# Graph attention layers on one core: s_j brought along the rows by way of memory, and the leaky scores made by ScalarE in PSUM

## The reference

```
h = max(layernorm(x), 0)
for l in range(3):
    si = h @ attn_w[l, :256];  sj = h @ attn_w[l, 256:]
    scores = si[:, :, None] + sj[:, None, :] + attn_b[l]
    scores = where(scores >= 0, scores, 0.2 * scores)      # leaky
    scores = where(adj + eye > 0, scores, -inf)
    attn = softmax(scores)
    h1 = layernorm(h + attn @ h) * g1[l] + beta1[l]
    h = layernorm(h1 + gelu(h1 @ W1[l] + b1[l]) @ W2[l] + b2[l]) * g2[l] + beta2[l]
out = x + h
```

## Time and profile before

| | before |
|---|---|
| median of 3 runs | 2236.1 us |
| the profiled execution | 2237.38 us, span 2235.3 us |
| busy: PE, PEld | 2193.7, 1525.4 us |
| busy: DVE, ACT, POOL | 1767.4, 1884.1, 1886.3 us |
| chain that ended last, by engine | PE 94%, POOL 2%, DVE 2%, ACT 1%, DMA 1% |
| chain, by line | L473 44%, L459 43%, L511 5%, L497 2% |
| DMA | 144.71 MB, mean 65 GB/s |

### The profile page before, as it was taken

One profiled execution on the slowest core, in us unless ns is written; L12 is line 12 of the kernel. 1 busy time (PEld: TensorE's weight loads), 2 busy tenths in 40 slices (PEclk: granted clock), 3 DMA queues, 4 the chain that ended last, 5 costly groups with the idle time before them and its releaser, 6 DMA issues.

```text
span 2235.3 us, 46173 instructions
## 1 busy us (share of the span) xinstructions
PE 2193.7 (98%) x15464; PEld 1525.4 (68%) x15464; DVE 1767.4 (79%) x5886; ACT 1884.1 (84%) x3496; POOL 1886.3 (84%) x1644
## 2 busy tenths in 40 slices
PE   4999999999999999999999999999999999999998
PEld 3667666666666766676667666666666676667665
DVE  7888787778887777778898777777898877777764
ACT  6898788889998888888999888888899888888874
POOL 5888788789998888788999887878899888878796
PEclk9999999999999999999999999999999999999999
DMA  5522212135542212124655122212455211221252
GB/s 150 133 65 53 57 34 39 32 61 101 118 108 56 34 35 39 34 39 72 124 101 108 39 39 34 39 32 43 86 114 122 52 35 34 39 34 39 53 95 67
DMA packets 382266, 144.71 MB, mean 65 GB/s; under 512 B 312144, under 2 KB 380368, under 8 KB 382032
## 3 DMA queue, kind: packets, MB, share of 16 engines
q1 hardware_dynamic: 366192, 126.04, 27.1%
q0 software_dynamic: 15840, 15.73, 4.9%
HBM read 49.96 MB, written 16.78 MB: 30 GB/s over the span
## 4 chain that ended last, share of the span: by engine, by line
PE 94%; POOL 2%; DVE 2%; ACT 1%; DMA 1%; issue 0%; DVEq 0%; POOLq 0%; ACTq 0%
PE p_pair L473 44%; PE p_hid L459 43%; PE p_pair L511 5%; PE p_pair L497 2%; DVE bn L719 0%; DMA hT_lo<-h_lo 0%; POOL rstd L984 0%; POOL h_lo L1002 0%; PE p_pair L484 0%; DVE dots L757 0%; POOL w_f L1028 0%; POOL X_lo L1006 0%; POOL w_f L1035 0%; DVE dots L760 0%; DMA x_in<-in_x 0%
## 5 line engine op out<-in xcount | busy, mean ns | idle before, releaser
L473 PE MATMUL p_pair<-w_hi,g_hi 128*128 128x256 f16 x3072 | 838.2, 273 | 0.0
L473 PE MATMUL p_pair<-w_lo,g_hi 128*128 128x256 f16 x3072 | 838.1, 273 | 0.0
L473 PE MATMUL p_pair<-w_hi,g_lo 128*128 128x256 f16 x3072 | 838.0, 273 | 0.0
L577 ACT ACTIVATE p_hid<-p_hid,b_eff 128x512 f32<-128x512 f32 x768 | 503.4, 655 | 285.7 <-PE p_hid L459 284.6
L712 DVE TENSOR_TENSOR g_lo<-p_hid,g_hi 128x512 f16<-128x512 f32 x768 | 527.3, 687 | 224.8 <-ACT g_hi L582 219.2
L582 ACT ACTIVATE g_hi<-p_hid 128x512 f16<-128x512 f32 x768 | 458.5, 597 | 24.4
L459 PE MATMUL p_hid<-hT_hi,w_hi 128*128 128x512 f16 x1536 | 458.2, 380 | 10.5 <-DVE g_lo L712 6.8
L984 POOL TENSOR_TENSOR rstd<-var_eps,minus_half 128x4 f32<-128x4 f32 x224 | 232.0, 1036 | 270.2 <-DVE minus_mean L727 269.9
L459 PE MATMUL p_hid<-hT_lo,w_hi 128*128 128x512 f16 x1536 | 458.4, 380 | 1.1 <-DMA hT_lo<-h_lo 1.1
L459 PE MATMUL p_hid<-hT_hi,w_lo 128*128 128x512 f16 x1536 | 458.7, 380 | 0.0
L473 PEld LDWEIGHTS p_pair<-w_hi,g_hi 128*128 128x128 f16 x3072 | 301.0, 98 | 106.9 <-issue 0.6
(11 more groups left out here) (77 smaller groups left out, 3487.5 us busy)
## 6 DMA issues: line engine op xcount, KB each, us to landing
out<-w_f SPq DMA_DIRECT2D x31, 512.0 KB, 3.8
x_in<-in_x SPq DMA_DIRECT2D x30, 512.0 KB, 6.6
w_f<-in_x POOLq DMA_DIRECT2D x30, 512.0 KB, 7.3
adj_in<-in_adj SPq DMA_DIRECT2D x32, 256.0 KB, 3.2
w_f<-in_L_gnn_W SPq DMA_DIRECT2D x6, 1024.0 KB, 7.1
hT_hi<-h_hi SPq DMA_TRANSPOSE x96, 3.1
hT_lo<-h_lo SPq DMA_TRANSPOSE x96, 3.0
pT_hi<-p_hi SPq DMA_TRANSPOSE x94, 2.4
```

Source lines behind the costliest of these rows:

```text
L473: mm = pe.matmul(ff_banks(s)[:, t, :], g[i][:, nodes], w[l][:, c, :], start=(c == 0 and t % 2 == 0 and n == 0), stop=(c == C - 1 and n == ...
L577: act.activation(p_hid[k][:], p_hid[k][:], ACT.Gelu, bias=b1_eff[:, l, c:c + 1], scale=1.0 / WSCALE).then_inc(gelu_ready, 1)
```

## The change

s_j of items 0 to 4 still comes from TensorE's transposes. For every later item SyncE writes s_j (128 nodes x 4 graphs, sixteen bytes a node) to a small tensor in memory at the beginning of a slot (`sj_to_memory`), and at the end of the slot reads it back, broadcast to all 128 partitions, 2 KB each (`sj_to_rows`), into the new tile sj_rows. ScalarE, in chunk 3 of the next slot, reads a graph's s_j out of sj_rows (every fourth value), adds s_i as the bias, applies the leaky slope and writes to PSUM, where the transposes used to write: four Prelu activations of 128x128 for an item. VectorE adds the mask to all four graphs in one instruction in chunk 4 and takes the row maxima, now directly as minus_max. The two ScalarE steps on leaky and minus_max go. So that s_j is there a slot earlier, dot products, input statistics and input normalization are done one item further ahead (s+5 and s+6 in place of s+4 and s+5). At the start inputs 4 and following are loaded into their X buffers. The bias of b2 is added to the residual rows by an accumulating DMA of POOL and no longer by VectorE. TensorE's bias folds of layers 1 and 2 use another bank half and stand in chunks 3 and 4.

ScalarE in a slot with an input normalization, before: from the gelu of chunk 3 to that of chunk 6 (p_hid is the hidden product, X the normalized input).

The diff, cut to its core:

```diff
+        sj_rows = sb("sj_rows", [P, N, T])
+        sj_memory = [nc.dram_tensor(f"sj_memory{i}", [N, T], F32).ap() for i in range(2)]
...
+            def sj_to_memory(r, s):
+                sp.wait_ge(dots_ready, total(r, s, 8, 8))
+                if later(r, s, 7):
+                    sp.wait_ge(sj_in, sj_total(r, s - 2))
+                sp.dma_start(sj_memory[s % 2], s_j[s % RING][:]).then_inc(sj_out, 16)
+
+            def sj_to_rows(r, s):
+                sp.wait_ge(sj_out, sj_total(r, s))
+                if later(r, s, 6):
+                    sp.wait_ge(leaky_ready, total(r, s - 1, 4, 4))
+                sp.dma_start(sj_rows[:].rearrange("p n t -> p (n t)"),
+                             sj_memory[s % 2].rearrange("n t -> (n t)").partition_broadcast(P)).then_inc(sj_in, 16)
+
             def slot(r, s):
+                if is_item(r, s + 4) and later(r, s, 2):
+                    sj_to_memory(r, s + 4)
                 if is_item(r, s + 2):
                     turn_probs_hi(r, s + 2)
                     turn_probs_lo(r, s + 2)
...
+                if is_item(r, s + 4) and later(r, s):
+                    sj_to_rows(r, s + 4)
...
             def aggregate(r, s):
...
-                    pe.wait_ge(score_steps, total(r, s + 1, 5, 4))
+                    pe.wait_ge(score_steps, total(r, s + 1, 2, 1))
...
-                    if c == 4 and is_item(r, s + 3):
-                        spread_sj(r, s + 3)
+                    if isinstance(r, int) and r == 0 and s < 2 and c == 4:
+                        spread_sj(0, s + 3)
...
-            def leaky_scores(r, s):
-                act.wait_ge(score_steps, total(r, s, 5, 5))
-
-                act.activation(minus_max[:], row_top[:], ACT.Prelu, scale=SLOPE, alpha=1.0 / SLOPE).then_inc(leaky_ready, 1)
-                act.activation(leaky[:], scores[:], ACT.Prelu, alpha=SLOPE).then_inc(leaky_ready, 1)
+            def leaky_scores(r, s, by_memory):
+                act.wait_ge(dots_ready, total(r, s, 8, 8))
+                if by_memory:
+                    act.wait_ge(sj_in, sj_total(r, s))
+                    act.wait_ge(res2_ready, total(r, s - 4, 2, 2))
+                else:
+
+                    act.wait_ge(sj_rows_ready, s + 1)
+                for t in range(T):
+                    rows = sj_rows[:, :, t] if by_memory else sj_bank(r, s)[:, t, :]
+                    act.activation(sj_bank(r, s)[:, t, :], rows, ACT.Prelu, alpha=SLOPE,
+                                   bias=s_i[s % RING][:, t:t + 1]).then_inc(leaky_ready, 1)
...
+                    if c == 3 and is_item(r, s + 3):
+                        leaky_scores(r, s + 3, later(r, s, 2))
                     if c == 2 and is_item(r, s + 1):
                         norm_attention(r, s + 1)
                     if c == 3 and is_item(r, s + 1):
                         high_h(r, s + 1)
...
-                    if c == 3 and is_item(r, s + 4) and layer_of(s + 4) == 0:
-                        norm_input(r, s + 4)
-                    if c == 5 and is_item(r, s + 3):
-                        leaky_scores(r, s + 3)
+                    if isinstance(r, int) and (r, s, c) == (0, 0, 3):
+                        norm_input(0, 4)
+                    if c == (4 if isinstance(r, int) and (r, s) == (0, 0) else 3) and is_item(r, s + 5) and layer_of(s + 5) == 0:
+                        norm_input(r, s + 5)
...
             def add_scores(r, s):
...
+                dve.wait_ge(leaky_ready, total(r, s, 4, 4))
+                if later(r, s):
+                    dve.wait_ge(probs_ready, total(r, s - 1, 4, 4))
+                dve.tensor_tensor(scores[:], sj_bank(r, s), mask[s % RING][:], ALU.add).then_inc(score_steps, 1)
...
-                    if c == 3 and is_item(r, s + 3):
+                    if c == 4 and is_item(r, s + 3):
                         add_scores(r, s + 3)
                         row_maxima(r, s + 3)
```

More of the change, by code:

```diff
@@ L299, in x_source @@
         def x_source(r, s):
-            return X[s] if isinstance(r, int) and r == 0 and s in (2, 3) else x_in[s % 2]
+            return X[s] if isinstance(r, int) and r == 0 and 2 <= s < RING else x_in[s % 2]
         block = ctx.enter_context(nc.Block())
@@ L320, in load_x @@
             def load_x(g):
-                dst = X[g] if g in (2, 3) else x_in[g % 2]
+                dst = X[g] if isinstance(g, int) and 2 <= g < RING else x_in[g % 2]
                 sp.dma_start(dst[:], graphs(x, g)).then_inc(x_loaded[g % 2], 16)
@@ L427, in opening @@
                 next_adj(4)
+                next_x(6)
                 turn_h_hi(0, 0)
@@ L617, in exponentials @@
                 for t in range(T):
-                    act.activation(probs[:, t, :], leaky[:, t, :], ACT.Exp, bias=minus_max[:, t:t + 1],
+                    act.activation(probs[:, t, :], scores[:, t, :], ACT.Exp, bias=minus_max[:, t:t + 1],
                                    accum_out=row_sum[:, t:t + 1]).then_inc(probs_ready, 1)
@@ L769, in add_scores @@
             def add_scores(r, s):
-                q = s % RING
-                dve.wait_ge(sj_rows_ready, total(r, s, 1, 1))
-                dve.wait_ge(dots_ready, total(r, s, 8, 8))
+                dve.wait_ge(leaky_ready, total(r, s, 4, 4))
                 if later(r, s):
-                    dve.wait_ge(leaky_ready, total(r, s - 1, 2, 2))
-                for t in range(T):
-                    dve.scalar_tensor_tensor(out=scores[:, t, :], in0=sj_bank(r, s)[:, t, :], scalar=s_i[q][:, t:t + 1],
-                                             in1=mask[q][:, t, :], op0=ALU.add, op1=ALU.add).then_inc(score_steps, 1)
+                    dve.wait_ge(probs_ready, total(r, s - 1, 4, 4))
+                dve.tensor_tensor(scores[:], sj_bank(r, s), mask[s % RING][:], ALU.add).then_inc(score_steps, 1)
             def row_maxima(r, s):
-                dve.wait_ge(score_steps, total(r, s, 5, 4))
-                dve.tensor_reduce(row_top[:], scores[:], AX.X, ALU.max, negate=True).then_inc(score_steps, 1)
+                dve.wait_ge(score_steps, total(r, s, 2, 1))
+                dve.tensor_reduce(minus_max[:], scores[:], AX.X, ALU.max, negate=True).then_inc(score_steps, 1)
             def row_sums(r, s):
@@ L849, in slot @@
             def slot(r, s):
-                first = isinstance(r, int) and (r, s) == (0, 0)
-                starts = is_item(r, s + 5) and layer_of(s + 5) == 0 and not first
+                starts = is_item(r, s + 6) and layer_of(s + 6) == 0 and not (isinstance(r, int) and (r, s) == (0, 0))
                 for c in range(C):
@@ L1067, in slot @@
                     low_X(r, s + 2)
+                if first:
+                    first_deviation(5, 0)
                 if is_item(r, s + 1):
```

114 lines of the change are left out of this document (62 added, 52 removed).

## The result

The changed kernel takes 2244.03 us (median of 7 runs, 2243.65 to 2246.04), the kernel before 2236.13 us on the same chip (2235.94 to 2237.1): ratio 1.0035, 95% interval 1.0023 to 1.0047. It is slower by 8 us, where I had forecast 12 us faster. The profiled execution has a span of 2242.0 us, 6.7 us more than before.

A forecast was written before the change was run, and what follows sets the result against it. TensorE's own instructions were taken to bound the kernel: 2237.4 - 40.0 (transposes removed) + 20.6 (aggregation waits) + 7 (opening) = 2225.0 us, 2224 on the runs' scale, with a range of 2203 to 2241.

The forecast's parts named there:

- TensorE's part: On TensorE, the four s_j transposes go for 91 items at 0.44 us each: 40.0 us less, all on the path.
- The new wait: In 24 slots normalizing an input, TensorE's aggregation waits for VectorE's mask addition, delayed by ScalarE's Prelus: 0.86 us each, 20.6 us.
- I take 0.29 us, 1.17 us for four: ScalarE, chunk 3: assumed start-to-start time of one added 128x128 Prelu, and of an item's four.
- I allow 0.1 us between the end of the releaser and TensorE's start: Estimated delay from the end of VectorE's mask addition to the start of TensorE's waiting aggregation.
- The start: Slots 0 and 1, ScalarE waiting for TensorE's late s_j transposes, and item 3's later statistics: 7 us more, bounds 2 to 12.
- The sum: Profiled 2237.4 - 40.0 + 20.6 + 7 = 2225.0 us; 2223.7 on the runs' scale, stated as 2224.
- An ordinary slot's slack: Without input normalization, masked scores would be ready 1.2 us before TensorE's aggregation needs them, so the Prelus are covered.
- Rival 1: The aggregation does not wait in slots with an input; at zero wait the time is 2203 us. Chance 0.15.
- Rival 3: s_j rows arrive late from memory, or their extra traffic delays transposes everywhere; 2269 us at half a microsecond in 90 slots. Chance 0.03.
- Rival 2: Slower: late transposed h_lo in slots normalizing an input (2246 us), or long Prelus (2243 us). Chance of both 0.15.
- first mechanism: Prelus delay the x_in load and the h_lo transpose queued behind it; TensorE waits in 24 slots, 21.7 us more, 2246 us.
- second mechanism: Each Prelu on ScalarE takes 0.49 us, lengthening the aggregation's wait by 0.78 us a slot: 18.8 us more, 2243 us.

## Why the prediction was wrong

- **TensorE's part**, -40.0 us: right. Ordinary slots are 22.15 us, and the spreads put back cost 40.7.
- **The new wait**, +20.6 us: the place, the releaser and the slots were right, and moving the normalization shows it. This is the term that was mis-sized: 1.52 us a slot and 36.4 us. Of the 0.66 too few, 0.48 is the step "I take 0.29 us, 1.17 us for four": a Prelu from sj_rows takes 0.41. My nearest row, the Exp, read a contiguous tile, and I did not look at how the new operand lies. The formula of the Trainium skill that I cited beside it ("ScalarE: Activation LUTs", What ACT_TABLE_LOAD costs) gives 0.293 and has no term for the layout either; the measured 0.41 decides. A further 0.16 is the step "I allow 0.1 us between the end of the releaser and TensorE's start", which is 0.26. Contiguous rows bring the slot to 23.17 us, still 0.16 above my 23.01, which is that release.
- **The start**, +7 us (its terms add up to 7.5): 10.3, which is 12.9 lost less 2.6 gained. The late spreads were in it, the weights in chunk 3 of slots 4 to 10 (3.2 us) were not. The bias folds, said to "cost what they cost now", cost 2.6 us less, and this hid a part of the loss. The weights meet the same chain as the input normalization, and the chain of the prediction, asked what else ever stands in chunk 3, would have given them.
- **The sum**: 2225.0 + 15.8 + 3.3 = 2244.1, against 2244.0 measured. This closes by construction, since the start's 10.3 is what is left of the span; it confirms nothing. The changed kernel's profiled execution equals its median, so of the 20.3 us between 2223.7 and 2244.0 the last 1.3 is the step that brought the sum to the runs' scale.
- **An ordinary slot's slack**, 1.2 us: too large. The doubled Prelus show 0.45 us. The difference is again the longer Prelus, 0.48, and the release, of which this sum had nothing: 1.18 - 0.48 - 0.26 = 0.44.
- **Rival 1**: no. **Rival 3**: no; the reads land in 3.8 us, and nothing waits for them.
- **Rival 2** was the right side. Its first mechanism, hT_lo, did not come in the changed kernel. That the slot grown by 1.52 us left it time is borne out in part: with contiguous rows the slots are 0.50 us shorter, and hT_lo ends last in four of them. It came in six slots when the wait was taken away and the load of x_in, moved behind the late normalization, held up the queue. Its second mechanism, the long Prelu, is what happened, with 0.41 us and not 0.49, and the rule of the Trainium skill named there, that an add belongs on VectorE, would have cost far more in this form, with both operands in SBUF beside a busy GpSimd: 2633 us.

The range's upper end, 2241, had no room for three misses of the same sign. The longer Prelu (24 x 0.48 = 11.5 us), the release (24 x 0.16 = 3.8) and the start (3.3) bring 2223.7 to 2242.3, and each of them comes from a different step.

## What to carry to other kernels

When work leaves the bounding engine, the next wait is found by writing down, for each kind of slot, everything that stands ahead of the releaser on its engine; then move what is not urgent behind it. Four instructions in another chunk were worth 31 us here, where the 364 operations taken from TensorE are worth 40. Price a new instruction by a row with the same layout of its operands, not only the same shape, and a new wait with the release between engines as measured.

## What the hardware showed

- ScalarE reading SBUF with a stride of sixteen bytes takes 0.11 us more over 128 columns (0.41 against 0.30), with eight bytes nothing, with thirty-two no more than with sixteen. VectorE pays 0.09 us at sixteen bytes; no other step was tried on it. For GpSimd the Trainium skill ("GPSIMD Engine Reference", Performance pitfalls for Q7 kernels) puts such a rise above steps of eight bytes; that the two other engines have one as well, these runs show.
- VectorE with two operands in SBUF waits for the whole of GpSimd's running operation: 2.41 us instead of 0.34. So does a strided single-source operation (267 ns alone, 2212 beside GpSimd).
- After 3.0 us without work TensorE's granted clock is 0.55 in the next 2.3 us, and it falls so behind 19 of the 24 waits of that length, not behind all. In the changed kernel, after the wait of 1.36 us before 1122.15, it is 1.00 in the 2.35 us that follow, and it falls behind none of the 24 such waits. It also fell once without a long wait: in the kernel before, at 226.30 to 231.00 us (0.64), where TensorE had waited 0.26 us at most in the 7.3 us before and 32 of its operations had been matmuls of one column.
- From the end of a VectorE operation to the start of a matmul that waits for it: 0.26 us, in all 24 slots with an input.
- Behind a DMA of 512 pieces of four bytes, with a load, a transpose and another load between them on the same queue, the issue of a transpose took 9.74 us instead of 1.24, once; that the pieces are the cause is not shown.
